# A decoder layer on one core: its prologue in another order, with one semaphore per stored projection

## The reference

```python
q, k, v = proj(Wq, bq), proj(Wk, bk), proj(Wv, bv)          # (4, 16, 1024, 16) each
attn = einsum('bhld,bhrd->bhlr', q, k) * scale
dist = clip(arange(L)[None, :] - arange(L)[:, None], -64, 8) + 64
rel = einsum('bhld,lrd->bhlr', q, dist_emb[dist]) * scale    # one of 73 vectors by distance
out = einsum('bhlr,bhrd->bhld', softmax(attn + rel), v)
x = layernorm(x + out @ Wo.T + bo)                           # then cross-attention, then the feed-forward part
```

## Time and profile before

| | |
|---|---|
| median of three runs | 1477.4 us |
| the profiled execution | 1474.41 us, span 1472.6 us |
| busy over the span | PE 87%, DVE 72%, ACT 64%, POOL 23% |
| DMA, the whole span | 260.55 MB, 177 GB/s |
| first score matmul (L812) | 151.04 us after the span's start |
| first score matmul of pass 1 | 177.51 us |

### The profile page before, as it was taken

One profiled execution on the slowest core, in us unless ns is written; L12 is line 12 of the kernel. 1 busy time (PEld: TensorE's weight loads), 2 busy tenths in 40 slices (PEclk: granted clock), 3 DMA queues, 4 the chain that ended last, 5 costly groups with the idle time before them and its releaser, 6 DMA issues. The chain is left out here.

```text
span 1472.6 us, 24890 instructions
## 1 busy us (share of the span) xinstructions
PE 1287.8 (87%) x8220; PEld 686.6 (47%) x8220; DVE 1066.9 (72%) x2589; ACT 940.4 (64%) x1650; POOL 337.0 (23%) x577
## 2 busy tenths in 40 slices
PE   8695899999999999999999999999995998810597
PEld 4342343344344334334434434437884787600486
DVE  4466778888877887887887888762663568999655
ACT  3331677777777777777777777773674559749600
POOL 3342112121121211212112121004552005600012
PEclk9897999999999999999999999999997999965799
DMA  8999886977877878788697786615411003316032
GB/s 246 275 296 263 224 213 196 262 210 207 238 203 233 217 218 225 206 247 209 198 257 211 214 227 181 199 73 168 115 58 44 1 1 129 135 51 228 0 111 90
DMA packets 260303, 260.55 MB, mean 177 GB/s; under 512 B 65838, under 2 KB 246606, under 8 KB 256078
## 3 DMA queue, kind: packets, MB, share of 16 engines
q1 hardware_dynamic: 260174, 258.95, 61.0%
HBM read 147.40 MB, written 110.71 MB: 175 GB/s over the span
## 5 line engine op out<-in xcount | busy, mean ns | idle before, releaser
L556 ACT ACTIVATE pr<-scoresT 128x512 f32<-128x512 f32 x1024 | 550.5, 600 | 217.9 <-PE scoresT L816 159.3
L812 PE MATMUL scoresT<-qT,kT 99*128 99x512 bf16 (+7 forms) x1408 | 359.0, 326 | 7.1 <-DMA qT<-sh 5.4
L659 DVE TENSOR_REDUCE mx<-scores_for_max 128x1 f32<-128x888 f32 (+6 forms) x448 | 301.5, 673 | 0.1
L654 DVE CUSTOM_DVE_ANT_0 junk<-scores_for_max,win 128x200 f32<-128x200 f32 (+2 forms) x512 | 179.9, 351 | 162.1 <-PE scores_for_max L787 154.5
L657 DVE TENSOR_REDUCE mx<-scores_for_max 128x1 f32<-128x64 f32 (+6 forms) x448 | 277.4, 619 | 0.1
L812 PEld LDWEIGHTS scoresT<-qT,kT 99*128 99x128 bf16 (+1 forms) x1408 | 113.6, 97 | 335.2 <-ACT rows L536 97.8
L829 PE MATMUL attn_out<-pr,vS 128*17 128x512 f32 x2048 | 269.5, 598 | 0.1
L816 PE MATMUL scoresT<-idf,win 128*128 128x128 f32 x1024 | 218.4, 274 | 0.0
L449 POOL COPY rows<-rows 128x736 f32<-128x736 f32 x128 | 102.1, 798 | 399.5 <-ACT rows L536 399.5
L786 PE MATMUL scores_for_max<-kX,qT 64*128 64x512 bf16 x512 | 165.7, 386 | 10.7 <-DVE mx L659 9.4
L787 PE MATMUL scores_for_max<-kX,qX 64*128 64x512 bf16 x512 | 165.6, 385 | 0.0
(11 more groups left out here) (204 smaller groups left out, 1778.0 us busy)
## 6 DMA issues: line engine op xcount, KB each, us to landing
rel_table<-rows SPq DMA_DIRECT2D x128, 512.0 KB, 4.5
win<-rel_table SPq DMA_DIRECT2D x128, 512.0 KB, 5.4
up_raw<-xT_normed SPq DMA_DIRECT2D x6, 1536.0 KB, 5.0
xT_normed<-up_raw SPq DMA_DIRECT2D x6, 1536.0 KB, 7.3
qT<-q_parts SPq DMA_DIRECT2D x32, 256.0 KB, 7.6
kX<-k_parts SPq DMA_DIRECT2D x64, 128.0 KB, 4.8
kT<-k_parts SPq DMA_DIRECT2D x32, 256.0 KB, 5.4
q_parts<-shared SPq DMA_DIRECT2D x32, 192.0 KB, 5.2
```

What stands on the lines that cost most here:

```text
L556: nc.scalar.activation(pr[:, n % NPR, h, :], bank, ACT.Exp).then_inc(t_read, 1)
L654: last = nc.vector.tensor_tensor_reduce(junk[:, n % 2, 0:z - a], bank[:, a:z], win[:, T % NW, q4, h, u:u + z - a], 1.0, NEG, ALU.add, ALU. ...
L659: last = nc.vector.tensor_reduce(mx[:, T % 2, q4, h, 2:3], bank[:, z:L], AX.X, ALU.max)
L812: last = mm(bank[:, a:e], k[0:r], q[0:r, a:e], start=(n == 0), stop=not near and n == len(pieces) - 1, skip_group_check=True)
```

## The change

q, k and v stores get a semaphore for each half and projection (`st_part[hf][n]`, `st_val[hf]`), and `high` and the value copy wait for their own alone. x of blocks 2 to 7 is loaded by ACT, behind `high(k, 0)`. The value step is divided: ACT copies the bank (two token tiles at once), POOL adds the bias. Rows and maxima come earlier, so that no chunks are left over. SP's order is written out. The first shift is made beside the last block: POOL behind step (6, 4), PE and ACT at (7, 0). SP's wait for all stores moves from before the loop to kt 1 of pass 0. The core of the diff:

```diff
@@ -108,8 +108,10 @@
         a_low = sem("a_low")
+        a_vc = sem("a_vc")
         a_v = sem("a_v")
-        a_out = [sem(f"a_out{j}") for j in range(2)]
+        st_part = [[sem(f"st_part{j}{n}") for n in range(4)] for j in range(2)]
+        st_val = [sem(f"st_val{j}") for j in range(2)]
         ld_q = [sem(f"ld_q{i}") for i in range(QS)]
@@ -179,7 +181,8 @@
         NCONST = 3 + 6
-        A_OUT = (14, 9)
+        PART_OUT = ((2, 2, 4, 4), (2, 2, 2, 2))
+        VAL_OUT = (2, 1)
@@ -211,12 +214,12 @@
         steps = [(k, n) for k in range(BLKS) for n in range(6)]
-        rows_after = {(3, 1 + j): (0, j) for j in range(4)}
-        rows_after.update({s_: (1, j) for j, s_ in enumerate(((3, 5), (4, 0), (4, 1), (4, 2)))})
-        rows_after.update({(5, 1 + j): (2, j) for j in range(4)})
+        rows_after = {s_: (0, j) for j, s_ in enumerate(((2, 4), (2, 5), (3, 0), (3, 1)))}
+        rows_after.update({(3, 2 + j): (1, j) for j in range(4)})
+        rows_after.update({(4, 2 + j): (2, j) for j in range(4)})
         first_chunks = [(0, c) for c in range(CH)] + [(1, c) for c in range(LEAD)]
-        chunk_after = dict(zip(steps[steps.index((4, 4)):], first_chunks))
-        chunks_left = first_chunks[len(chunk_after):]
+        chunk_after = dict(zip(steps[steps.index((4, 0)):], first_chunks))
+        SHIFT_STEP = (7, 0)
@@ -236,8 +239,6 @@
             def load_x(k):
-                if k >= 2:
-                    sp.wait_ge(a_full, 6 * (k - 1))
                 sp.dma_start(xs[:, k % 2], xT[:, k * HALF:(k + 1) * HALF].rearrange("(c p) n -> p c n", p=P)).then_inc(a_x[k % 2], 16)
@@ -260,17 +261,17 @@
                     src = part[gg * G * HD:(gg + 1) * G * HD, hf, n]
-                    sp.dma_start(dst[:, :, cols], src).then_inc(a_out[hf], 16)
+                    sp.dma_start(dst[:, :, cols], src).then_inc(st_part[hf][n], 16)
                     if n >= 2 and hf == 0:
-                        sp.dma_start(dst[:, :, L:L + WRAP], src[:, :, 0:WRAP]).then_inc(a_out[hf], 16)
+                        sp.dma_start(dst[:, :, L:L + WRAP], src[:, :, 0:WRAP]).then_inc(st_part[hf][n], 16)
...
                 sp.wait_ge(a_v, 2 * k + 2)
-                sp.dma_start(vd[b, cols].rearrange("(t p) c -> p t c", p=P), vs[:, hf].rearrange("p t h r -> p t (h r)")).then_inc(a_out[hf], 16)
+                sp.dma_start(vd[b, cols].rearrange("(t p) c -> p t c", p=P), vs[:, hf].rearrange("p t h r -> p t (h r)")).then_inc(st_val[hf], 16)
                 if hf == 0:
-                    sp.dma_start(vd[b, L:L + WRAP], vs[0:WRAP, hf, 0].rearrange("p h r -> p (h r)")).then_inc(a_out[hf], 16)
+                    sp.dma_start(vd[b, L:L + WRAP], vs[0:WRAP, hf, 0].rearrange("p h r -> p (h r)")).then_inc(st_val[hf], 16)
@@ -336,61 +337,77 @@
                                  zero[:, :].rearrange("p (t n) -> p t n", n=P)).then_inc(s_pads, 16)
-            for k in range(2):
-                for n in range(4):
+            def stored(n, k):
+
+                for hf in range(2):
+                    sp.wait_ge(st_part[hf][n], 16 * PART_OUT[hf][n] * ((k - hf) // 2 + 1))
+
+            def store_parts(k, *projections):
+                for n in projections:
                     store_part(k, n)
-                if k == 0:
-                    store_values(k)
-                load_x(k + 2)
-            for hf in range(2):
-                sp.wait_ge(a_out[hf], 16 * (A_OUT[hf] - hf))
+
+            def store_rows(T, *tiles):
+                for j in tiles:
+                    store_row(T, j)
+
+            store_parts(0, 0, 1, 2, 3)
+            store_values(0)
+            store_parts(1, 0, 1, 2, 3)
+            stored(0, 1)
             load_q(0)
             store_values(1)
-            for k in range(2, BLKS):
-                for n in range(4):
-                    store_part(k, n)
-                    if k == 3 and n >= 2:
-                        store_row(0, n - 2)
-                    if k == 4:
-                        store_row(1, n)
-                    if k == 5 and n >= 2:
-                        store_row(2, n - 2)
-                    if k == 6 and n < 2:
-                        store_row(2, 2 + n)
+            store_parts(2, 0, 1)
+            stored(2, 1)
+            load_max_operands(0)
+            store_parts(2, 2)
+            store_rows(0, 0)
+            store_parts(2, 3)
+            store_rows(0, 1)
+            store_values(2)
+            store_parts(3, 0)
+            store_rows(0, 2, 3)
+            store_parts(3, 1)
+            sp.wait_ge(s_pads, 16 * 2 * G)
+            load_windows(0)
+            load_q(1)
+            store_rows(1, 0)
+            store_parts(3, 2)
+            store_rows(1, 1)
+            store_parts(3, 3)
+            store_rows(1, 2, 3)
+            store_values(3)
+            store_parts(4, 0, 1)
+            load_windows(1)
+            store_rows(2, 0)
+            store_parts(4, 2)
+            store_rows(2, 1)
+            store_parts(4, 3)
+            store_rows(2, 2, 3)
+            store_values(4)
+            load_k(0)
+            sp.wait_ge(s_bufs, 1 + 2 * G)
+            for par in range(2):
+                sp.dma_start(kT[99:102, par, :, (TL - 1) * P:L - WRAP], none[0:3, :, 0:P - WRAP]).then_inc(s_wrap, 16)
+            for k in range(5, BLKS - 1):
+                store_parts(k, 0, 1, 2, 3)
                 store_values(k)
-                if k + 2 < BLKS:
-                    load_x(k + 2)
-                if k == 4:
-                    sp.wait_ge(s_bufs, 1 + 2 * G)
-                    for par in range(2):
-                        sp.dma_start(kT[99:102, par, :, (TL - 1) * P:L - WRAP], none[0:3, :, 0:P - WRAP]).then_inc(s_wrap, 16)
-                if k == 2:
-                    load_max_operands(0)
-                    load_q(1)
-                if k == 3:
-                    store_row(0, 2)
-                    store_row(0, 3)
-                    sp.wait_ge(s_pads, 16 * 2 * G)
-                    load_windows(0)
-                if k == 4:
-                    load_windows(1)
-                    load_k(0)
-                if k == 5:
-                    load_max_operands(1)
+            place_shift(0)
+            load_windows(2)
+            load_max_operands(1)
+            sp.wait_ge(a_full, 6 * (BLKS - 1) + 4)
             for hf in range(2):
-                sp.wait_ge(a_out[hf], 16 * A_OUT[hf] * B)
-            sp.wait_ge(a_full, 6 * BLKS)
+                sp.wait_ge(st_val[hf], 16 * VAL_OUT[hf])
             load_v(0)
-            place_shift(0)
+            store_parts(BLKS - 1, 0, 1, 2, 3)
+            store_values(BLKS - 1)
...
                     sp.wait_ge(t_full, entries_to("score", T - 1, 4 * TL - 1))
-                if T + 2 < NT:
-                    if T:
-                        sp.wait_ge(x_read, CH * T)
-                        sp.wait_ge(m_ready, T)
+                if T and T + 2 < NT:
+                    sp.wait_ge(x_read, CH * T)
+                    sp.wait_ge(m_ready, T)
                     load_windows(T + 2)
@@ -400,6 +417,11 @@
                         ahead.load(sp)
+                    if kt == 1 and T == 0:
+                        for n in range(4):
+                            stored(n, BLKS - 1)
+                        for hf in range(2):
+                            sp.wait_ge(st_val[hf], 16 * VAL_OUT[hf] * B)
                     if kt == 1 and T % 2 == 0:
@@ -444,6 +466,12 @@
+            def add_value_bias(k, v):
+                pool.wait_ge(a_vc, 2 * k + v + 1)
+                to = vs[:, k % 2, 2 * v:2 * v + 2, :, 0:HD]
+                nc.gpsimd.tensor_tensor(to, to, bvt[:].rearrange("p (h d) -> p h d", d=HD).unsqueeze(1).to_broadcast([P, 2, NH, HD]),
+                                        ALU.add).then_inc(a_v, 1)
+
             def pad_row(T, j):
@@ -480,14 +508,18 @@
             for k, n in steps:
+                if (k, n) == (0, 4):
+                    pool.wait_ge(s_const, 16 * NCONST)
+                    pool.wait_ge(s_ones, 1)
                 if n < 4:
                     low(k, n)
+                else:
+                    add_value_bias(k, n - 4)
                 if (k, n) in rows_after:
                     pad_row(*rows_after[k, n])
-            for hf in range(2):
-                pool.wait_ge(a_out[hf], 16 * A_OUT[hf] * B)
-            shift_of(0)
-            cut_window(0)
+                if (k, n) == (6, 4):
+                    shift_of(0)
+                    cut_window(0)
             for T in range(NT):
@@ -513,8 +545,8 @@
                 hf = k % 2
-                if k >= 2 and n == 0:
-                    act.wait_ge(a_out[hf], 16 * A_OUT[hf] * (k // 2))
+                if k >= 2:
+                    act.wait_ge(st_part[hf][n], 16 * PART_OUT[hf][n] * (k // 2))
                 act.wait_ge(a_full, 6 * k + 1 + n)
@@ -522,6 +554,18 @@
                 nc.scalar.activation(part[:, hf, n, 1, :], rem[:, hf, n, :], ACT.Copy).then_inc(a_mid, 1)
+
```

(57 more changed lines are left out.)

## The result

The changed kernel takes 1463.56 us (median of four runs, 1462.73 to 1464.41) against 1477.79 us of the kernel before in the same runs: ratio 0.9907, 95% interval 0.9890 to 0.9924, so 14 us or 0.9% faster. The forecast was 1464. The profiled execution took 1462.73 us, its span 1460.9 us.

The account below looks back on a forecast made before the run. Transfers were taken to bound the prologue after 42 us: 42 + 115.4 + 6 of waits + 1 for the shift starts pass 1 at 164.4 against 177.5, 13 us earlier; 1464.4 against the median, range 1450 to 1474.

Parts of the forecast that it names:

- The bound: Prologue up to shift 1: the same transfers, 161.6 us of all 16 engines, set when pass 1 begins, 13 us earlier.
- The rate: From 42 us to shift 1: 124.6 us of transfers pass at 1.08 in 115.4, plus three SP waits of 2 us.
- The sign I had given: Prologue into pass 0: DMA share of 1.05 or more from 60 to 160 us.
- The first score and pass 0: First score matmul at 125 to 131 us, then a wait of 3 to 10 us for vS or the shift.
- Window 0: Prologue, window load: issued 9.8 us earlier, at 66 us; DVE's wait for it ends at 72 to 77 us.
- the x loads on ACT: Prologue, six loads: PE's wait for x goes, issuing costs ACT at most 1.4 us each, nothing saved at the DMA bound.
- The values and rows: Prologue: ACT copies at 0.69 us and POOL adds at 1.2 us, hidden; rows moved up three or five steps.
- The wait for row (0,0): Prologue, block 3: PE or ACT still waits 6 to 10 us near 50 us for this row's store.
- A: Rival, prologue: the engines set the pace, needing a share of 1.18; 23 us earlier, 1454 from the median; chance 0.23.
- B: Rival, prologue: transfers keep the old share of 1.00, pass 1 at 169.6; 8 us earlier, 1469; chance 0.17.
- C: Rival, prologue: waits only move a block up, sole gain the idle 141 to 150 us; 0 to 4 us; chance 0.08.
- D: Rival, pass 0: SP's new wait for block 7's stores delays shift 1; 13 us later, 1490; chance 0.05.

Follow-up runs that it names:

- both edits: Changed kernel with the load of vS 0 issued straight after shift 0 and SP's wait for block 7's stores moved to pass 2: 1462.09 us, ratio 0.9886.

## Why the prediction was right

**The bound.** "Exactly the same transfers precede shift 1 in both kernels": the sum was put at 161.6 and measures 159.9, and in the last table it is 158 to 163 in ten orders. What shows the bound is that adding 3.1 MB moved pass 1 by 5.8 to 6.3 us, and that taking vS's wait away moved it by nothing. This was the step on which the forecast of 13 us and not 23 rested, and it is shown.

**The rate.** Two terms were off and met. From 42 us on the work was 122.1 us where I had 124.6, and it took 122.1 where I had 121.4 (and 1 for the shift). I had it as 1.08 throughout plus three waits of 2 us. What happened: 1.08, 1.07 and 1.04 in the full stretches and 6 us at 0.67 for window 0. SP's wait for block 7's stores, 4.6 us long (142.3 to 146.9), shows in the last of these stretches as 3 us at 0.69 (147 to 150), some 1.2 us of the engines. The wait before window 1 cost nothing (1.09 from 81 to 84 us). In its place stand 12 us at 0.65 from 117 to 129 us, where SP issued small transfers without a pause. That stretch alone is 12 x (1.08 - 0.65) = 5.2 us of the engines; no step of mine had it. The sign I had given, a share of 1.05 or more from 60 to 160 us, failed with it: it was 1.00. That the forecast came within half a us of the median is therefore luck; the bound earned the direction and the rough size, 13 us and not 23.

**The first score and pass 0.** Forecast 128 (125 to 131), measured 129.56; forecast waits of 3 to 10 us in pass 0 for vS or the shift, measured 4.2 and 1.2, and with the lower clock behind the first wait (a granted 0.71 on the mean from 141 to 150 us), pass 0 took 8.0 us more. No step of mine had the clock. Window 0 released DVE at 72.9 (72 to 77 given). I overlooked what is late next there: q of group 1 behind it, until 76.85.

**x.** Its wait is gone, as forecast; landing took 4.7 to 7.7 us, and ACT paid 0.37 to 0.43 us an issue, under the 1.4 allowed. What I missed is its worth: put back, it costs 5.1 us at pass 1, where the prediction had the x loads on ACT save nothing at the DMA bound. Together with the tail, 9.0 us if undone, this is more than the whole 13.4, so the parts don't add up; rows and maxima moved up, and the finer semaphores, were not tried by themselves, and what they give by themselves is open.

**The values and rows.** ACT's copies took 0.59 to 0.60 us (0.69 taken), POOL's adds 1.18 (1.2 taken), both hidden. The wait for row (0,0) was put at 6 to 10 us near 50 us; it is 4.8 at 55.5, with four smaller ones behind it.

**The rivals.** A needed a mean share of 1.18; it was 1.00. That is B's rate, and not the 1.03 that the forecast's 124.6 in 121.4 us comes to. B and the forecast are one mechanism, and the forecast hit the number with 2.5 us too much work against a rate 0.03 too high; B, at 169.6, missed 164.1 by that work and by 3 us of waits counted on top. C gave at most 4 us and is out with 13.4 at pass 1. D, SP's wait in pass 0, was worth about 1 us. The rule of the Trainium skill (DMA: Bandwidth & Descriptors, Issuing engines are not separate DMA queues) that a second issuer saves only issuing time and adds no rate agrees with the trace: 1.07 to 1.09 in unbroken backlog with one queue or with two. That time was not small here: SP's issuing was the limit from 117 to 129 us, and giving ACT four transfers of 6 KB lifted that stretch from 0.67 to 0.89.

## What to carry to other kernels

Where the transfers are the bound, sum their busy share up to the first instruction that needs the last of them: that sum stays when the order changes, and only its idle gaps, and the transfers queued ahead that could stand behind, can be won. When a wait for one transfer is removed, look for the next one in the same queue before pricing the gain. Price a long wait of PE with the clock behind it: here 8 us of waiting cost 2.3 us more. Read a lead some passes behind the point that was moved, and not at it. A mean share of 0.75 in a loop says nothing of slack for what is queued last in each pass.

## What the runs showed of the hardware

Issuing limited the transfers: with 0.61 to 0.82 us for each DMA, small ones (3 and 6 KB) between stores of 192 KB held the 16 engines at a share of 0.65 for 12 us. A transfer on ACT's queue passed SP's backlog, though not at once (7.8 us against 4.7 without backlog). Loads of few, long rows ran at 156 GB/s at a share of 1.01 (57 to 60 us before), stores and windows at 380. Where loads and stores ran mixed, the share went above 1.1 (1.14 from 141 to 150 us with both edits in pass 0; 1.20, at 218 GB/s, from 138 to 141 us in the changed kernel), so a share of 1.09 is no ceiling for every mix.

After a wait of 7.7 to 8.3 us before pass 1, in three kernels, PE was granted 0.50, the level of 1.2 GHz, in the first 5 us of pass 1, and the next shift's copy came 2.3 us later behind the start of the pass than in the kernels with waits of 0.7 to 1.6 us there, which were granted 1.00.
